# A transformer layer on one core: the opening before the first round is rearranged (stores of the split parts, weight staging, checks, flag)

## The reference

```
x = x + attention(layernorm(x))    # 16 heads of 16; rotary q and k; a key j <= i counts if it is in the
                                   # same block of 64, at most 128 back, or one of the first 4; then out_w
x = x + ffn(layernorm(x))          # h = silu(w1 x * s1) * (w2 x * s2), 1024 wide
                                   # h = gelu(h1 h * s), h = gelu(h2 h * s), then w3 h * s3
```

## Time and profile before

| | |
|---|---|
| time, median of 3 runs | 1177.59 us |
| time of the profiled execution | 1174.98 us |
| its span, first to last instruction | 1173.2 us |
| mean granted TensorE clock | 0.966 |
| busy: TensorE matmul, VectorE, ScalarE, GpSimd | 1074.2, 639.1, 717.6, 470.4 us |
| first `scores` of sequence 0 starts | 60.33 us |
| first `gated_tile` starts | 162.37 us |
| last matmul starts | 1169.86 us |

### The profile page before, as it was taken

One profiled execution on the slowest core, in us unless ns is written; L12 is line 12 of the kernel. 1 busy time (PEld: TensorE's weight loads), 2 busy tenths in 40 slices (PEclk: granted clock), 3 DMA queues, 4 the chain that ended last, 5 costly groups with the idle time before them and its releaser, 6 DMA issues.

```text
span 1173.2 us, 21628 instructions
## 1 busy us (share of the span) xinstructions
PE 1074.2 (92%) x7538; PEld 885.2 (75%) x7538; DVE 639.1 (54%) x1986; ACT 717.6 (61%) x1774; POOL 470.4 (40%) x656
## 2 busy tenths in 40 slices
PE   4166669999999999999999999999999999999998
PEld 2144568788977888778977888777977889888987
DVE  3068525755656556665556555755466555565422
ACT  1445535856767855857657756758558656867422
POOL 6233123723535334624526334625327224324433
PEclk9677889999999999999999999999999999999999
DMA  9777755784547365465447465464456464431540
GB/s 300 232 198 240 216 159 162 221 282 145 187 117 241 103 198 162 150 196 158 153 131 232 124 188 163 150 209 126 130 177 198 144 180 158 131 109 55 183 141 18
DMA packets 138269, 198.54 MB, mean 169 GB/s; under 512 B 7856, under 2 KB 90032, under 8 KB 138160
## 3 DMA queue, kind: packets, MB, share of 16 engines
q1 hardware_dynamic: 138160, 197.14, 54.6%
HBM read 155.16 MB, written 49.28 MB: 174 GB/s over the span
## 4 chain that ended last, share of the span: by engine, by line
PE 74%; ACT 9%; DVE 4%; SPq 4%; DMA 4%; issue 3%; POOL 2%; POOLq 0%; ACTq 0%; DVEq 0%
PE bank L709 34%; PE bank L679 11%; PE bank L733 4%; PE bank L516 4%; PE bank L575 4%; PE bank L618 4%; PE bank L587 3%; PE bank L595 3%; ACT Sm L855 2%; PE bank L540 2%; SPq L370 2%; PE bank L641 2%; POOL a_lo L1288 2%; ACT L875 2%; ACT a_hi L876 1%
## 5 line engine op out<-in xcount | busy, mean ns | idle before, releaser
L855 ACT ACTIVATE Sm<-Sm,smin 128x260 f32<-128x260 f32 (+2 forms) x512 | 241.4, 473 | 187.2 <-DVE smin L1037 186.8
L709 PE MATMUL bank<-b_hi,W 128*128 128x512 f32 x512 | 214.9, 420 | 1.1 <-POOL b_lo L1288 1.1
L709 PE MATMUL bank<-a_hi,W 128*128 128x512 f32 x512 | 208.1, 407 | 0.1
L709 PE MATMUL bank<-b_lo,W 128*128 128x512 f32 x512 | 202.1, 395 | 0.0
L709 PE MATMUL bank<-a_lo,W 128*128 128x512 f32 x512 | 200.9, 392 | 0.0
L1052 DVE COPY PT<-bank 128x512 f32<-128x512 f32 x128 | 88.1, 688 | 134.1 <-PE bank L618 118.8
L679 PE MATMUL bank<-x_hi,W 128*128 128x256 f32 x512 | 126.4, 288 | 8.6 <-issue 8.6
L679 PE MATMUL bank<-x_lo,W 128*128 128x256 f32 x512 | 124.7, 285 | 0.0
L1297 POOL TENSOR_TENSOR a_lo<-a_act,a_hi 128x256 fp32r<-128x256 f32 x128 | 94.4, 740 | 75.4 <-ACT a_hi L902 75.4
L1288 POOL TENSOR_TENSOR a_lo<-a_act,a_hi 128x512 fp32r<-128x512 f32 x64 | 81.0, 1292 | 82.1 <-ACT a_hi L876 82.1
L1037 DVE CUSTOM_DVE_ANT_0 Sm<-bank,msk,gmin 128x256 f32<-128x256 f32 x256 | 108.2, 478 | 9.6 <-PE bank L575 9.5
(11 more groups left out here) (110 smaller groups left out, 2178.6 us busy)
## 6 DMA issues: line engine op xcount, KB each, us to landing
W<-w_scratch SPq DMA_DIRECT2D x168, 512.0 KB, 4.2
qk_scratch<-split SPq DMA_DIRECT2D x128, 256.0 KB
Qs<-qk_scratch SPq DMA_DIRECT2D x128, 128.0 KB, 5.2
Ks<-qk_scratch SPq DMA_DIRECT2D x16, 1024.0 KB, 8.9
w_scratch<-in_ffn_w SPq DMA_DIRECT2D x22, 512.0 KB, 7.4
stage_a<-in_ffn_w SPq DMA_DIRECT2D x16, 512.0 KB, 8.2
x_in<-in_x SPq DMA_DIRECT2D x8, 512.0 KB, 10.3
x<-in_x SPq DMA_DIRECT2D x8, 512.0 KB, 4.1
```

The costliest lines, as they stand in the source:

```text
L709: mm = nc.tensor.matmul(bank[n % 2][:, :], lhsT.bitcast(F32) if general else lhsT, rhs, start=(kk == 0 and part == 0), stop=(kk == NH - 1 ...
L855: ex = nc.scalar.activation(row, row, ACT.Exp, bias=smin[:, r, c:c + 1], scale=-1.0, accum_out=rowsum[:, i % 2, col:col + 1])
```

## The change

The rounds 0 to 7 keep their order. What changes is the following.

- `save_split` makes 2 stores of 512 KB for each f and kind in place of 4 of 256 KB, in all rounds. The destination's outer dimension is now the 128 partitions, with 2 rows of 2 KB in each. Before, it was 8 groups of 16 rows.
- The parts of half f = 1 of sequence 0 go to a second tile, `split_first`, which lies in the memory of PT. `keep_cur(0, 0)` waits until it has been stored.
- SP no longer stages weights. ScalarE's queue issues 2 MB, 2 MB and 2 MB (h1 and w1, w2) after x has landed, in rows of 16 KB, and in steps 1, 3, 5, 7 and 9 four transfers of 1 MB (h2) and one of 1 MB (w3) with rows of 8 KB. GpSimd gathers all 8 slots from them, 4 in round -2 and 4 in steps 1 to 4.
- out_w, x1, the scales and s3 are loaded in steps 2 and 4. The first layernorm and projections of sequence 1 run 3 steps later (SHIFT), with a MISC order of their own (OPENING), and so do their splits and stores, at steps 9, 11, 12 and 13 of SP. GpSimd's second-layernorm application of tiles 0 and 1 waits for steps 14 and 15.
- Checks are spread: 4 in round -2, then at steps 2, 4, 11 and 13 of ScalarE. `low_bits` stands at step 14 of VectorE.
- The flag is read between steps 15 and 16 of TensorE. Steps 16 to 19 are part of the two copies; the v projection of sequence 1 uses banks 0 and 1, one tile behind each of steps 16 to 19. The copy for exact weights now comes first, behind `If`.
- The first 4 copies to `w_scratch` are issued in steps 14 and 15.

```diff
-Q_PARTS, K_PARTS = (0, 0, 1, 1), (2, 3, 2, 3)
-SAVES = PARTS
+SAVES = 2
...
+SHIFT, KNOWN = 3, UNITS
...
+OPENING = ("t0", "t1", "qk0", "qk1", "o0", "qk2", "qk3", "gs", "o1", "pg0", "o2", "n0", "pg1", "n1", "n2", "o3",
+           "vg", "n3")
...
+        split_first = sb("split_first", [P, 4, SEQ], F32R, at=pt_at)
...
+        def v_bank(b, t):
+            if b == 1:
+                return bank[t // 2][:, t % 2 * EMB:(t % 2 + 1) * EMB]
+            return bank[4 + t % 2][:, 0:EMB]
+        def parts_of(b, f):
+            return split_first if (b, f) == (0, 1) else split
...
-                rows = qk_scratch[b % 2][f][kind].rearrange("s (e a d) c -> a s e d c", e=2, a=PARTS)
-                for part, source in enumerate((Q_PARTS, K_PARTS)[kind]):
-                    sp.dma_start(rows[part].rearrange("s e d c -> (s e) d c"),
-                                 split[:, source, :].bitcast(F32)).then_inc(split_saved[f][kind], 16)
+                rows = qk_scratch[b % 2][f][kind].rearrange("s (p i j) c -> i j (s p) c", i=2, j=2)
+                for source in range(2):
+                    dst = rows[:, source] if kind else rows[source]
+                    sp.dma_start(dst.rearrange("r p c -> p r c"), parts_of(b, f)[:, 2 * kind + source, :].bitcast(F32)
+                                 .unsqueeze(1).broadcast_to([P, 2, SEQ])).then_inc(split_saved[f][kind], 16)
...
-            def stage_late(j):
-                sp.wait_ge(low_summed, j // 2 + 1)
-                sp.wait_ge(w_placed, j + 1)
-                src = chunk_of_weights(OTHERS[EARLY + j])
-                sp.dma_start(stage_a[:, j, :].rearrange("p (k o) -> p k o", o=src.shape[2]), src)\
-                    .then_inc(late_loaded[j], 16)
...
+                    if r == -1:
+                        if n in (9, 11, 12, 13):
+                            save_split(1, n // 12, int(n in (11, 13)))
+                        if n == 2:
+                            sp.dma_start(out_w[:, :, :], outT).then_inc(out_loaded, 16)
+                            load_x1(0)
+                        if n == 4:
+                            sp.dma_start(scales[:, :, :], ffn_s).then_inc(attn_loaded, 16)
+                            sp.dma_start(s3[:, :], s3row.broadcast_to([P, EMB])).then_inc(attn_loaded, 16)
+                        if n == 12:
+                            load_x(2)
+                        if n >= 14:
+                            save_weights(OTHERS[2 * n - 28])
+                            save_weights(OTHERS[2 * n - 27])
...
+            sp.dma_start(msk[:, :, :], mask).then_inc(msk_loaded, 16)
+            for kind in range(2):
+                save_split(0, 0, kind)
+            for kind in range(2):
+                save_split(0, 1, kind)
             for f in range(NF):
-                for kind in range(2):
-                    save_split(0, f, kind)
-            load_first_stacks(0)
+                load_queries(0, 0, f)
+                load_keys(0, f)
             load_x(1)
-            load_x1(0)
...
+                    if b == 1:
+                        if t == 0:
+                            pe.wait_ge(low_ready, 1)
+                    elif t < 2:
...
+                    elif s == 2:
+                        pe.wait_ge(v_kept, 2 * NT * 2)
...
+            def beside_attention(r, general, first=0):
+                for n in range(first, STEPS):
                     step(r, n, general)
+                    if r == -1 and n >= UNITS:
+                        v_projection(r, [n - UNITS])
                 if has_q(r):
-                    v_projection(r)
+                    if r >= 0:
+                        v_projection(r)
...
-            beside_attention(-1, False)
-            pe.wait_ge(low_found, 1)
-            nc.tensor.matmul(bank[0][0:1, 0:1], low_all[:, :], minus_half, start=True, stop=True)\
-                .then_inc(low_added, 1)
+            for n in range(KNOWN):
+                if n == KNOWN - 1:
+                    pe.wait_ge(low_found, 1)
+                    nc.tensor.matmul(bank[0][0:1, 0:1], low_all[:, :], minus_half, start=True, stop=True)\
+                        .then_inc(low_added, 1)
+                step(-1, n, False)
             pe.wait_ge(low_ready, 1)
-            low_bits = pe.value_load(low_int[0:1, 0:1], min_val=0, max_val=1)
+            exact = pe.value_load(exact_int[0:1, 0:1], min_val=0, max_val=1)
             def rounds(general):
+                beside_attention(-1, general, KNOWN)
...
-            with pe.If(low_bits):
+            with pe.If(exact):
+                rounds(False)
+            with pe.Else():
                 rounds(True)
-            with pe.Else():
-                rounds(False)
...
+                if (b, f) == (1, 0):
+                    act.wait_ge(split_saved[0][kind], 16 * SAVES)
+                elif b:
+                    act.wait_ge(split_saved[1 - f][kind], 16 * SAVES * (b + f))
...
+            def stage_later(n):
+                if n == 1:
+                    act.wait_ge(low_summed, SLOTS // 2)
+                    act.wait_ge(w_placed, 4)
+                if n in (1, 3, 5, 7):
+                    j = n // 2
+                    act.dma_start(stage_a[:, 2 * j:2 * j + 2, :].rearrange("p s c -> p (s c)"),
+                                  ffn_w[:, W_H2 + 2 * j * SLOT:W_H2 + 2 * (j + 1) * SLOT]).then_inc(h2_staged[j], 16)
+                if n == 9:
+                    act.dma_start(stage_b[:, 4:6, :].rearrange("p s c -> p (s c)"), ffn_w[:, W_DN:W_DN + 2 * SLOT])\
+                        .then_inc(dn_staged, 16)
...
+                    if r == -1 and n in (2, 4):
+                        check_weights(SLOTS // 2 + n // 2 - 1)
+                    if r == -1 and n == 11:
+                        check_weights(CHECKS - 1)
+                    if r == -1 and n == 13:
                         check_weights(CHECKS)
...
+            act.wait_ge(x_loaded, 16)
+            for n in range(2):
+                act.dma_start(stage_a[:, 4 * n:4 * n + 4, :].rearrange("p s c -> p (s c)"),
+                              ffn_w[:, W_H1 + 4 * n * SLOT:W_H1 + 4 * (n + 1) * SLOT]).then_inc(h1_staged[n], 16)
+            act.dma_start(stage_b[:, 0:4, :].rearrange("p s c -> p (s c)"), ffn_w[:, W_UP:W_H1]).then_inc(up_staged, 16)
             keep_xnT(-2, 0)
             keep_xnT(-2, 1)
-            for n in range(2 * NF):
-                split_hi(-2, n)
-                if n:
-                    check_weights(n - 1)
+            split_hi(-2, 0)
+            split_hi(-2, 1)
+            check_weights(0)
+            split_hi(-2, 2)
+            check_weights(1)
+            split_hi(-2, 3)
             keep_v(-2)
-            for n in range(2 * NF - 1, CHECKS):
-                check_weights(n)
+            check_weights(2)
+            check_weights(3)
+            beside_attention(-1)
...
+                if a == 0 and n == 0:
+                    for kind in range(2):
+                        dve.wait_ge(split_saved[1][kind], 16 * SAVES)
...
+                    nq = n if r >= 0 else n - SHIFT
+                    if r == -1 and n == 14:
+                        low_bits()
...
+                    if r == -1 and n == KNOWN - 1:
+                        no_low_bits()
...
+                        if r == -1 and n in (14, 15):
+                            ln2_apply(a, n - 14)
...
+                if slot in UP_SLOTS:
+                    pool.wait_ge(up_staged, 16)
+                    j = UP_SLOTS.index(slot)
+                    src = stage_b[:, 0:4, j * 2 * P:(j + 1) * 2 * P]
+                else:
+                    for n in range(2):
+                        pool.wait_ge(h1_staged[n], 16)
+                    src = stage_a[:, :, slot * P:(slot + 1) * P]
+                nc.gpsimd.tensor_copy(W[:, slot, :].rearrange("p (k o) -> p k o", o=src.shape[2]), src).then_inc(w_placed, 1)
...
+                    if r == -1 and n in (1, 2, 3, 4):
+                        place_weights(UP_SLOTS[n - 1])
...
```

More of the change, by code:

```diff
@@ L218, in layer_kernel @@
         rope_loaded = sem("rope_loaded")
+        msk_loaded = sem("msk_loaded")
+        out_loaded = sem("out_loaded")
         attn_loaded = sem("attn_loaded")
@@ L221, in layer_kernel @@
         w_loaded = [sem(f"w_loaded{n}") for n in range(SLOTS)]
-        stage_loaded = [sem(f"stage_loaded{n}") for n in range(CHECKS)]
-        late_loaded = [sem(f"late_loaded{n}") for n in range(SLOTS)]
+        h1_staged = [sem(f"h1_staged{n}") for n in range(2)]
+        up_staged = sem("up_staged")
+        dn_staged = sem("dn_staged")
+        h2_staged = [sem(f"h2_staged{n}") for n in range(NH // 2)]
         w_placed = sem("w_placed")
@@ L481, in misc_free @@
                 else:
-                    order = [u for u in ROUND if has_q(r) or u[0] in "opn"]
+                    order = [u for u in (ROUND if r >= 0 else OPENING) if has_q(r) or u[0] in "opn"]
                     n = order.index(name)
@@ L529, in global_scores, with v_projection @@
```

(29 more changed lines are left out.)

114 lines of the change are left out of this document (49 added, 65 removed).

## The result

Four runs of the changed kernel gave 1144.92 to 1148.02 us, median 1145.95. Four of the kernel before, on the same chip, had a median of 1175.82. The ratio is 0.9749, with a 95% interval of 0.9730 to 0.9767: 29.5 us, or 2.5%, faster. The profiled execution took 1148.02 us (before: 1174.98), its span is 1146.1. The forecast of 1150.0 lies 4.1 us above the median, and the range held it.

A forecast was written before the change was run, and what follows sets the result against it. TensorE was taken to bound the rounds; a chain of stores, the load of x and an unexplained 8.43 us the opening. Six terms summed to -27.6 us, from 1174.98 to 1147.4; plus 2.6 for the median: 1150.0, range 1137 to 1168.

The forecast's parts named there:

- Term A: Opening up to the first scores: 60.33 us would fall to about 41, a gain of 19.3 us.
- 46 if the stores stay at 205: Upper bound for the first scores: 46 us if the 4.2 MB of stores still moved at 205 GB/s, taking 20.5 us.
- two causes named for the 14.48 us: Split of q, half 1, waited for a store to free its buffer: weights ahead in SP's queue, no tile of its own.
- Term B: Steps 0 to 3 of the opening: 14.93 us would fall to 10, a gain of 4.9 us.
- Term C: Steps 4 to 11: 44.66 us would become 46.4, 1.7 longer, from 38.4 of VectorE work plus four waits.
- Term D: Steps 12 to 15: 16.03 us would become 18.4, 2.4 longer, with VectorE newly waiting for ScalarE's last check.
- Term E: From step 16 to the first gated tile: 26.42 us would fall to 17.9, a gain of 8.5 us.
- 3.4 us left for the switch: At the flag: of 8.43 us of silence, 5 would go with the copy right behind the test and 3.4 stay.
- Term F: End of the kernel: the copy for exact weights must jump over the other, costing 1 us.
- the steps wait more: Rival: MISC's order and the stores chain the engines, C reaches 55 and D 22, +12 us, 1162; chance 0.12.
- ScalarE is held by its own transfers: Rival: issuing 6.3 MB holds ScalarE 18 us, its first copy comes 14.4 us late, +29 us, 1179; chance 0.06.
- slow the rounds: Rival: new stores ahead of weights in SP's queue delay six rounds by 7 us each, 42 us, 1192; chance 0.05.

The follow-up runs named there:

- e5: Changed kernel with the second tile for the parts of half 1 undone, so its split waits for the other half's store; ratio 0.9748 to the kernel before.
- e10: Changed kernel without the shift of sequence 1 and with ScalarE's last check in step 12; ratio 0.9721 to the kernel before.
- e6: Changed kernel with the first 6 MB of weights on ScalarE's queue in short pieces of 512 bytes and 1 KB; ratio 0.9880 to the kernel before.
- e9: Changed kernel with the first 6 MB of weights issued by SP behind the mask, in the same long rows; ratio 0.9744 to the kernel before.
- e3: Changed kernel with the old 4 stores of 256 KB put back in all rounds; ratio 0.9883 to the kernel before.
- e4: Kernel before with the 2 new stores of 512 KB alone; ratio 0.9889 to the kernel before.
- e7: Changed kernel with sequence 1 not shifted and its stores at SP's steps 6, 8, 9 and 10; ratio 0.9726 to the kernel before.
- e8: Changed kernel with SP's store of k, half 0, one step earlier and ScalarE's last check in step 12; ratio 0.9713 to the kernel before.
- e1: Changed kernel with the copy for exact weights put second again, so the switch jumps over the other copy; ratio 0.9823 to the kernel before.
- e2: Kernel before with only the copy for exact weights put first, behind If; ratio 0.9945 to the kernel before.

## Why the prediction was right

**What bounds the kernel.** The rounds kept their order and their 1007.5 us. All that the trace shows of the gain lies ahead of 133.46. That the two lengths agree to 0.03 us is luck. Three stretches of TensorE's work, before, after and in e5, with the granted clock as the third number from the end:

```profile
162.37:165.95 3.58, 3.58 (x17) 3.58 (x18) 0.48 (x1) 0.48 (x1) 0.00 (x0) 0.50 0.02 5
```

```profile
204.70:208.10 3.40, 3.40 (x14) 2.91 (x14) 2.28 (x10) 0.94 (x4) 0.96 (x2) 0.50 1.04 331
```

```profile
204.70:208.10 3.40, 3.40 (x21) 2.82 (x20) 2.56 (x11) 1.57 (x7) 1.14 (x5) 1.00 1.00 308
```

Before, the rounds began with 3.58 us at 0.50, behind the silence, and had one more such stretch of 3.41 us later. After, they began at 1.00 but had two stretches of 3.41 us, at 204.7 and 607.5. e5 and e10 had none and took 1004.3. With half of the time at 0.50 taken off, the rounds of all fourteen kernels are 1003.7 to 1004.5 us long. So before the change the head of the rounds lost 1.8 us more, to a clock that had fallen during the silence, and a second later stretch in the profile after hid that gain.

**Term A was right, its bound was not.** The forecast was 41 and the trace has 41.66. Both assumed mechanisms were shown: the rate of the new stores (335 GB/s against 201) and the release of the issuing queue (e6, e9). But the upper bound "46 if the stores stay at 205" counted bytes alone. e3 measured 52.23, since slow stores also hold SP in issuing and the loads of the stacks stand behind them. And of the two causes named for the 14.48 us of the earlier trace rows, only one needed a cure: with fast stores issued early the second tile is worth nothing measurable (e5). The row of 378 GB/s at 1.07, taken as that of the Ks loads, also has a copy to `w_scratch` in it; e4 is the better evidence.

**Term B was right** (10.22 for 10), with TensorE at 0.50 in this stage (1.2 GHz). That it is a gain of its own is only half true: e7 shows that the shift moves some of this work to stage C.

**Term C was mis-sized, +4.9 for +1.7.** VectorE's work was 1.4 us more than forecast (39.82 for 38.4), and its idle time 1.7 us more (49.55 - 39.82 = 9.7, for waits of 8). For step 8 the forecast had 2 us of waiting for o0 behind the rotation of qk1. The trace has ScalarE's split of k waiting 4.59 us for GpSimd, and GpSimd had the second layernorm's step (L1285) ahead of this rotation, where it waited 9.00 us for VectorE's statistics:

```profile
77.88 0.57 POOL L1285 TENSOR_SCALAR ve<-mv 128x1 f32<-128x1 f32 x1 [9.00 <-DVE mv L1140]
```

The forecast named GpSimd only for step 4. No run took this wait away, so its share in the stage is argued. The wait for the store of SP's step 11 was put at 2.5 and measured 4.24 us. For step 12, where gs and o1 meet, the forecast had 2.5. These are VectorE's timeline rows at that store and at step 12:

```profile
96.67 0.69 DVE L1054 SCALAR_TENSOR_TENSOR split<-k,split 128x512 fp32r<-128x512 f32 x1 [1.53 <-ACT split L860]
102.57 0.48 DVE L1101 CUSTOM_DVE_ANT_0 Sm<-bank,msk,gmin 128x256 f32<-128x256 f32 x1 [2.39 <-PE bank L592]
```

That place was sized right. The wait for the store was on the chain and could be had for nothing: without it step 12 starts 4.6 us earlier (e8).

**Term D was right in kind.** The wait for the check stands at step 14 as forecast, 3.17 us long for 1.8, while the stage as a whole came out 0.9 us shorter than forecast.

**Term E was mis-sized, -11.9 for -8.5.** The mechanism was right: it is the jump to a copy that isn't at hand (e1, e2). The 3.4 us left for the switch were too many: with the copy right behind the test 0.65 us of idle time remain, and 1.16 from the flag (1.17 in e2). Nearly the whole silence was the jump's, not only the part up to the fetched block, and that is 2.75 us of the difference; the rest of the stage took 13.85 us for 14.5. The Trainium skill's rule (Runtime: NRT & Kernel Launch, "Instruction fetch mechanics") is that a taken branch whose target is not among the blocks at hand has to fetch it by DMA before it can go on. The traces agree: 7.65 to 8.43 us from the flag to the next work with a block fetched in between, 1.15 to 1.20 with none.

**Term F** measured +1.8 for +1.0, and not by the mechanism forecast: it is not TensorE that is late. In after TensorE's last instruction of its own begins at 1142.62, but SP waits for the last output store until 1145.7. These are the instruction blocks and the last store (KB, us from issue to landing) in after from 1141 to 1146, and the store before, from 1169.9 to 1173.2, where no block is fetched:

```profile
q8 instruction: 1, 0.02, 1.6%
y<-y_acc SPq DMA_DIRECT2D x1, 128.0 KB, 3.5
```

```profile
y<-y_acc SPq DMA_DIRECT2D x1, 128.0 KB, 1.7
```

Of the eleven kernels with the jump at the end (after and all but e1 and e4), nine show 4.4 to 5.4 us there. By the packet records of the traces, in each of these nine 135 of the store's 144 packets end 2.6 us behind the start of the last matmul, as before the change; the other 9, a sixteenth, start only when the instruction block ends, and are through 0.7 us later. e5 and e6 fetch a block too, but none of their packets waits for it, and they show 3.3 us, as the three kernels without the jump do. So the price, 0 to 2 us, is that of a block in the way of a sixteenth of the last store; why it is in the way in nine kernels and not in two stays open.

**Errors that cancel.** C's +3.2 against E's -3.4 is why the sum came out within 0.5 us. The profiled execution was forecast at 1147.4 us and took 1148.02; the median missed by 4.1 us because it was put 2.6 us above the profiled execution, as before the change, and lay 2.1 below it. The rival "the steps wait more" was right about C's direction and wrong about its size (49.55, not 55). "ScalarE is held by its own transfers" is a true mechanism, but for short rows only (e6). The new stores didn't slow the rounds: 1007.52 us.

## What to carry to other kernels

A queue that issues many transfers in 512-byte pieces is itself an engine on the path: look at how long its issues hold it, and at the DMA share while only one kind of transfer runs; a share of 0.53 with bytes waiting was here a matter of the stores' layout, not of the memory. Undo the parts of a combined change one at a time, and don't add up what they give: here the stores, the row length and the order of two code copies held nearly all of the gain and overlapped, and the second tile and the shift gave nothing measurable. Before comparing the length of a stage in two profiles, compare its granted clock. When work is moved into steps that are nearly full, follow every engine's own order past it, GpSimd's too, since the engine with the least work may be the one that is late.

## What the runs showed that was not expected

- Which of two code copies stands right behind a test is worth 6.5 to 8.7 us in the middle of a kernel with full DMA traffic. The jump over the other at the end costs 0 to 2 us, and not on TensorE: a fetched instruction block holds up 9 packets of the last output store.
- The issue of 4 MB in 512-byte pieces held an engine 12.92 us, in rows of 16 KB 0.86 us.
- The rounds took between 1004.3 us (e5, e10) and 1010.0 us (e4) in the profiled executions, with unchanged work in them. The granted clock accounts for it: a stretch of 3.41 us at 0.50 adds about 1.7 us; e5 and e10 had none in the rounds, after had two, and e4 had two and 5.84 us at the start. The timed runs of one kernel follow the clock as well (e10: 1139.51 us at a mean of 0.988, 1145.85 at 0.975), which is a reason why gains of 3 us in the opening don't show in the timed ratios. Why such a stretch comes in one execution and not in another is not shown.
